# A GRU over 256 steps: the output product in one piece of 256 columns, ahead of the loop's jump

## The chip, the cores and the metric

The kernel runs on one core of a Trainium2 chip. The metric is the device time of one execution in microseconds. All data are fp32.

## What is computed

A recurrence over T = 256 steps for B = 32 sequences with C = 256 channels, and a residual:

```python
def step(H, xs):
    xz, xr, xh = xs
    Z = sigmoid(xz + H @ Whz.T + bhz)
    R = sigmoid(xr + H @ Whr.T + bhr)
    H_tilda = tanh(xh + R * H @ Whh.T + bhh)
    H_new = Z * H + (1.0 - Z) * H_tilda
    Y = H_new @ Whq.T + bhq
    return (H_new, Y)
# xz, xr, xh: x @ Wx.T + bx for the gates z, r and h, of every step
_, Ys = scan(step, h0, (Xz, Xr, Xh))
out = x + transpose(Ys, (1, 0, 2))
```

## The kernel before

States are held transposed, channels on the 128 partitions in K = 2 halves and 32 sequences along the free axis (h_sb, rh_sb, zh_sb, u_sb, z_sb). Steps are taken in chunks of CS = 2. The loop runs NIT = 64 times over SLOTS = 4 steps, u = 0 to 3, that is two chunks, p = 0 and 1; s is the step in the chunk (even steps s = 0, odd steps s = 1). PSUM banks hold the sums before the nonlinearity: r_ps and c_ps (two each), z_ps and y_ps (one for each p). ScalarE seeds each with its bias (seed, seed_y), TensorE adds products to it.

In a step (names as in the code): r is the sigmoid of r_ps (L182), rh = r * h on VectorE (L232), z the sigmoid of z_ps (L186), zh = z * h (L237), the tanh of c_ps (L193), u = (1 - z) * tanh (L240), the new h = zh + u (L245).

Every product is cut in four strips of 32 output rows (`columns`, L254, and `y_piece`): four matmuls with 128 x 32 weights at tile_position (0, 32 j) that lie side by side in the array. What TensorE gets is, in each step:

- r of this step. As h = zh + u, the parts (k, o) of `Whr h` are taken by distributivity: three parts from zh at the end of the step before (AHEAD), three from u as soon as it is there, and the last from h. A part is a half k of the input by a half o of the output. The first step of the loop, u = 0, is different: only one part comes from zh and one from u, three from h.
- z from h (16 matmuls), c from rh (16 matmuls, behind the waits s_rh).
- x pieces: the x products of the *next* chunk, moving 64 columns (two steps). 12 for a chunk, six in each step: one of the gate N ahead of z, one N and one Z ahead of c, one Z and two R behind c.
- the r parts from zh for the step to come (behind the wait s_zh).
- a y piece: one half k of the output product of the *last* chunk, both steps of it. Here h is the stationary operand and whq_sb moves with 128 columns. Its four strips are half and step: partitions are (half of C, step, sequence), columns 128 channels. Both pieces add up in PSUM.

The loop's jump stands behind the y piece of u = 3. VectorE adds y_ps and the rows of x (xres_sb) to o_sb in even steps, ahead of zh (`residual`, L219), and SP sends o_sb out and fetches new x and new rows. y_ps is seeded by ScalarE in odd steps between z and tanh (L190). Everything is ordered by hand; each engine runs its own copy of the loop, and semaphores link them.

## Time and profile before

| | us |
|---|---|
| median of 3 runs | 521.46 (520.5 to 522.43) |
| profiled execution | 522.41 |
| its span, first to last instruction | 520.6 |

| engine | busy us | share |
|---|---|---|
| TensorE matmuls | 508.4 | 98% |
| TensorE weight loads | 491.0 | 94% |
| ScalarE | 322.4 | 62% |
| VectorE | 306.6 | 59% |

DMA moves 53 GB/s in the mean. The chain of work that ended last is 96% TensorE. Matmuls are pipelined and their ends are modelled, so their starts are to be read rather than their durations: a matmul record is 0.19 to 0.29 us long, while the next four start a few hundredths of a microsecond later. A line of the timeline is a run of like instructions; its second number is the time from the first start to the last end.

### The profile page before, as it was taken

To read this page: it belongs to the slowest core of one execution; us is meant where nothing else is said; L and a number is where in the kernel's file an instruction comes from. 1 tells how busy PE (TensorE), PEld (TensorE's weight loads), DVE (VectorE), ACT (ScalarE), POOL (GpSimd) and SP (SyncE) were. 2 spreads that over 40 slices of the span, in tenths; PEclk is the share of its full clock that TensorE was granted. 3 is DMA by queue.
4 is the path that set the end of the run, shared out by engine and by line. 5 is a ranking of instruction groups with operands and counts; after the bars stand their busy time and mean duration, and the time that the engine had idled before them with its cause. 6 is when DMAs were issued, how large, how long until landed. Compare 5 with 4: busy or idle time off the path is not lost.

```text
span 520.6 us, 96194 instructions
## 1 busy us (share of the span) xinstructions
PE 508.4 (98%) x44184; PEld 491.0 (94%) x44184; DVE 306.6 (59%) x1929; ACT 322.4 (62%) x1800; POOL 0.2 (0%) x4
## 2 busy tenths in 40 slices
PE   8499999999999999999999999999999999999997
PEld 7499999999999999999999999999999999999997
DVE  1256666666666666666566666666666666665664
ACT  2256666666666666666666666666666666666664
POOL 0000000000000000000000000000000000000000
PEclk9989999999999999999999999999999999999999
DMA  5011111111111111111211111111111111111111
GB/s 182 25 45 49 52 51 50 51 50 50 50 50 50 52 49 50 55 46 50 55 46 50 55 47 50 54 50 50 51 50 50 50 50 50 50 50 52 49 50 52
DMA packets 57737, 27.64 MB, mean 53 GB/s; under 512 B 6785, under 2 KB 56833, under 8 KB 57729
## 3 DMA queue, kind: packets, MB, share of 16 engines
q1 hardware_dynamic: 56880, 26.70, 18.3%
q10 hardware_dynamic: 848, 0.83, 0.5%
q8 instruction: 6, 0.10, 0.1%
q14 instruction: 3, 0.02, 0.0%
HBM read 18.98 MB, written 8.52 MB: 53 GB/s over the span
## 4 chain that ended last, share of the span: by engine, by line
PE 96%; issue 2%; DMA 1%; SPq 0%; DVE 0%; ACT 0%; ACTq 0%; DVEq 0%
PE r_ps L252 34%; PE c_ps L252 27%; PE z_ps L252 24%; PE y_ps L252 11%; DMA whq_sb<-in_whq_dram 1%; SPq L117 0%; SPq L119 0%; SPq L118 0%; SPq L115 0%; DVE h_sb L245 0%; DVE o_sb L219 0%; DVE rh_sb L232 0%; DVE u_sb L240 0%; ACT c_ps L193 0%; ACT y_ps L182 0%
## 5 line engine op out<-in xcount | busy, mean ns | idle before, releaser
L252 PE MATMUL c_ps<-xt_sb,wx_sb 128*32 128x64 f32 (+1 forms) x4104 | 174.4, 225 | 1.3 <-issue 1.3
L252 PE MATMUL z_ps<-xt_sb,wx_sb 128*32 128x64 f32 (+1 forms) x4104 | 168.1, 221 | 0.5 <-issue 0.5
L232 DVE TENSOR_TENSOR rh_sb<-y_ps,h_sb 128x32 f32<-128x32 f32 x512 | 89.7, 192 | 130.0 <-ACT y_ps L182 130.0
L182 ACT ACTIVATE y_ps<-r_ps 128x32 f32<-128x32 f32 x512 | 87.3, 182 | 98.4 <-PE r_ps L252 92.2
L252 PE MATMUL z_ps<-h_sb,whz_sb 128*32 128x32 f32 x8192 | 124.2, 198 | 2.2 <-issue 2.2
L252 PE MATMUL c_ps<-rh_sb,whh_sb 128*32 128x32 f32 x8192 | 123.0, 198 | 2.0 <-issue 1.9
L252 PE MATMUL y_ps<-whq_sb,h_sb 128*32 128x128 f32 x2064 | 112.2, 278 | 0.2 <-DVE h_sb L245 0.2
L252 PE MATMUL r_ps<-xt_sb,wx_sb 128*32 128x64 f32 (+1 forms) x4104 | 112.3, 220 | 0.0
L252 PEld LDWEIGHTS z_ps<-h_sb,whz_sb 128*32 128x32 f32 x8192 | 109.0, 111 | 2.4 <-issue 2.4
L252 PEld LDWEIGHTS c_ps<-rh_sb,whh_sb 128*32 128x32 f32 x8192 | 103.5, 110 | 2.3 <-issue 2.0
L252 PEld LDWEIGHTS z_ps<-xt_sb,wx_sb 128*32 128x32 f32 (+1 forms) x4104 | 104.6, 110 | 0.7 <-issue 0.7
L252 PEld LDWEIGHTS r_ps<-u_sb,whr_sb 128*32 128x32 f32 x5120 | 86.1, 112 | 15.9 <-DVE u_sb L240 15.9
L252 PEld LDWEIGHTS c_ps<-xt_sb,wx_sb 128*32 128x32 f32 (+1 forms) x4104 | 98.1, 108 | 1.5 <-issue 1.5
L252 PE MATMUL r_ps<-zh_sb,whr_sb 128*32 128x32 f32 x5120 | 94.0, 197 | 1.9 <-issue 1.9
L252 PE MATMUL r_ps<-u_sb,whr_sb 128*32 128x32 f32 x5120 | 94.4, 197 | 0.3
L252 PEld LDWEIGHTS r_ps<-xt_sb,wx_sb 128*32 128x32 f32 (+1 forms) x4104 | 84.3, 110 | 0.2 <-issue 0.2
L252 PE MATMUL r_ps<-h_sb,whr_sb 128*32 128x32 f32 x3080 | 82.7, 199 | 0.0
L252 PEld LDWEIGHTS r_ps<-zh_sb,whr_sb 128*32 128x32 f32 x5120 | 75.1, 112 | 2.0 <-issue 2.0
L237 DVE TENSOR_TENSOR zh_sb<-z_sb,h_sb 128x64 f32<-128x64 f32 x256 | 57.0, 223 | 31.0 <-ACT z_sb L186 30.9
L245 DVE TENSOR_TENSOR h_sb<-zh_sb,u_sb 128x32 f32<-128x32 f32 x512 | 75.0, 187 | 0.0
L186 ACT ACTIVATE z_sb<-z_ps 128x64 f32<-128x64 f32 x256 | 57.2, 223 | 27.3 <-PE z_ps L252 27.0
L240 DVE SCALAR_TENSOR_TENSOR u_sb<-z_sb,c_ps 128x32 f32<-128x32 f32 x256 | 48.0, 188 | 39.2 <-ACT c_ps L193 32.9
(29 smaller groups left out, 438.1 us busy)
## 6 DMA issues: line engine op xcount, KB each, us to landing
xt_sb<-in_xt_dram SPq DMA_DIRECT2D x130, 64.0 KB, 1.7
xres_sb<-in_xr_dram SPq DMA_DIRECT2D x130, 64.0 KB, 1.8
out_dram<-o_sb SPq DMA_DIRECT2D x130, 64.0 KB, 1.6
wx_sb<-in_wx_dram SPq DMA_DIRECT2D x3, 256.0 KB, 3.2
whr_sb<-in_whr_dram ACTq DMA_DIRECT2D x1, 256.0 KB, 5.3
whz_sb<-in_whz_dram ACTq DMA_DIRECT2D x1, 256.0 KB, 5.5
...
```

Of the source, the lines that this page charges most:

```text
L182: nc.scalar.activation(r_out[p][o], r_ps[:, o, here], ACT.Sigmoid).then_inc(s_r[o], 1)
L186: nc.scalar.activation(z_sb[:], z_view(p)[:, :, B * s:B * s + B], ACT.Sigmoid).then_inc(s_z, 1)
L232: nc.vector.tensor_tensor(rh_sb[:, k], r_out[p][k], old[:, k], ALU.mult).then_inc(s_rh[k], 1)
L237: nc.vector.tensor_tensor(zh_sb[:], z_sb[:], old, ALU.mult).then_inc(s_zh, 1)
L240: nc.vector.scalar_tensor_tensor(u_sb[:, k], z_sb[:, k], 1.0, c_out[p][k], ALU.subtract, ALU.mult, reverse0=True).then_inc(s_u[k], 1)
L245: nc.vector.tensor_tensor(new[:, k], zh_sb[:, k], u_sb[:, k], ALU.add).then_inc(s_h[k], 1)
L252: return nc.tensor.matmul(ps, weights, moving, start=start, stop=False, skip_group_check=True, **kw)
```

## The change

y of a chunk is made once, in the odd step, by four matmuls with 256 moving columns (`y_rows`). The strips are now half k of h and step: the two halves' sums lie on the partitions 0 to 63 and 64 to 127 of y_ps, rows (step, sequence), columns all 256 channels. VectorE adds them in two operations of 64 x 256: the first half and the rows of x in the even step (behind rh, ahead of zh), the second half in the odd step. bq_sb, xres_sb, o_sb and the DRAM tensors change their shapes with it; bq is zero on the second half's partitions, and its transfer grows from 64 to 128 KB. ScalarE's seed of y moves behind the tanhs of even steps.

TensorE's order: y stands ahead of the r parts from zh in odd steps. At u = 3 it is the last thing before the jump, and the r parts from zh come behind the jump, at the head of the loop, behind a semaphore of their own (s_zh_pass). The step u = 0 splits r as the others do. x pieces are dealt out 8 to the even and 4 to the odd step.

```diff
+ROWS = CS * B
-AHEAD = [((1, 0),)] + [((0, 0), (1, 0), (1, 1))] * (SLOTS - 1)
+AHEAD = ((0, 0), (1, 0), (1, 1))
+AT_R = ((N, 0),), ((N, 2),)
+AT_Z = ((N, 1), (Z, 0)), ((N, 3), (Z, 3))
+AT_N = ((Z, 1), (Z, 2), (R, 0), (R, 1), (R, 2)), ((R, 3),)
...
 # ScalarE
-                return nc.scalar.copy(y_ps[p][:, 0, 0:P], bq_sb[:])
+                return nc.scalar.copy(y_ps[p][:, 0, 0:C], bq_sb[:])
...
-            seed_y(1).then_inc(s_seed_y, CS)
...
-                    if s == CS - 1:
-                        act.wait_ge(s_rh[1], t + 1)
-                        seed_y(p).then_inc(s_seed_y, CS)
                     for o in range(K):
                         act.wait_ge(s_c_ps[o], t + 1)
                         nc.scalar.activation(c_out[p][o], c_ps[:, o, here], ACT.Tanh).then_inc(s_c[o], 1)
-                    if s == CS - 1:
+                    if s == 0:
+                        act.wait_ge(s_res, t + CS)
+                        seed_y(1 - p).then_inc(s_seed_y, CS)
+                    else:
...
+            act.wait_ge(s_res, T + CS)
+            seed_y(1).then_inc(s_seed_y, CS)
...
 # VectorE
+            def residual_half0(p, row_dmas):
                 dve.wait_ge(s_rows[p], row_dmas)
-                dve.wait_ge(s_y_ps, chunk + PAD + 1)
-                nc.vector.tensor_tensor(o_sb[:, p], y_ps[p][:, 0, 0:P], xres_sb[:, p], ALU.add).then_inc(s_res, CS)
+                nc.vector.tensor_tensor(o_sb[:, p], y_ps[p][0:ROWS, 0, 0:C], xres_sb[:, p], ALU.add).then_inc(s_half, CS)
+
+            def residual_half1(p, count):
+                dve.wait_ge(s_half, count)
+                nc.vector.tensor_tensor(o_sb[:, p], y_ps[p][ROWS:P, 0, 0:C], o_sb[:, p], ALU.add).then_inc(s_res, CS)
...
 # TensorE
+            def y_rows(p):
                 for j in range(NQ):
-                    half, step = divmod(j, CS)
-                    last = mm(y_ps[p][B * j:B * j + B, 0, 0:P], h_sb[:, k, CS * p + step], whq_sb[:, k, P * half:P * half + P],
+                    k, step = divmod(j, CS)
+                    last = mm(y_ps[p][B * j:B * j + B, 0, 0:C], h_sb[:, k, CS * p + step], whq_sb[:, k],
                               tile_position=(0, B * j))
...
                     if u == 0:
-                        pe.wait_ge(s_u[1], done)
-                        r_part(u, 1, 0, u_sb[:, 1])
-                        pe.wait_ge(s_h[0], done)
-                        r_part(u, 0, 0, old[:, 0]).then_inc(s_r_ps[0], 1)
-                        r_part(u, 0, 1, old[:, 0])
-                        pe.wait_ge(s_h[1], done)
-                        r_part(u, 1, 1, old[:, 1]).then_inc(s_r_ps[1], 1)
-                    else:
...
+                        pe.wait_ge(s_zh_pass, done)
+                        for k, o in AHEAD:
+                            r_part(u, k, o, zh_sb[:, k])
...
                     if s == CS - 1:
                         x_mm.then_inc(s_xt_used, 1)
-                    pe.wait_ge(s_zh, done)
-                    for k, o in AHEAD[(u + 1) % SLOTS]:
-                        r_part((u + 1) % SLOTS, k, o, zh_sb[:, k])
-                    if s == 0:
                         pe.wait_ge(s_seed_y, done)
-                    y_mm = y_piece(q, s)
-                    if s == CS - 1:
-                        y_mm.then_inc(s_y_ps, 1)
+                        y_rows(q).then_inc(s_y_ps, 1)
+                    if u < SLOTS - 1:
+                        pe.wait_ge(s_zh, done)
+                        for k, o in AHEAD:
+                            r_part(u + 1, k, o, zh_sb[:, k])
```

What this does to TensorE's row round the jump: first the head of the loop (u = 0, up to the first x piece), then, behind the "...", its end (u = 3, from the c matmuls of rh's second half on). Before:

```order
L252 MATMUL r_ps<-u_sb,whr_sb 32x32 [waits s_u1]
L252 MATMUL r_ps<-u_sb,whr_sb 32x32 x3
L252 MATMUL r_ps<-h_sb,whr_sb 32x32 [waits s_h0]
...
L252 MATMUL c_ps<-rh_sb,whh_sb 32x32 x7
L252 MATMUL z_ps<-xt_sb,wx_sb 32x64 x4
L252 MATMUL r_ps<-xt_sb,wx_sb 32x64 x8
L252 MATMUL r_ps<-zh_sb,whr_sb 32x32 [waits s_zh]
L252 MATMUL r_ps<-zh_sb,whr_sb 32x32 x3
L252 MATMUL y_ps<-whq_sb,h_sb 32x128 x4
L314 REGISTER_ALU
L314 COMPARE_AND_BRANCH
```

The same places of TensorE after the change:

```order
L279 MATMUL r_ps<-zh_sb,whr_sb 32x32 [waits s_zh_pass]
L279 MATMUL r_ps<-zh_sb,whr_sb 32x32 x11
L279 MATMUL r_ps<-u_sb,whr_sb 32x32 [waits s_u0]
L279 MATMUL r_ps<-u_sb,whr_sb 32x32 x3
L279 MATMUL r_ps<-u_sb,whr_sb 32x32 [waits s_u1]
...
L279 MATMUL c_ps<-rh_sb,whh_sb 32x32 x7
L279 MATMUL r_ps<-xt_sb,wx_sb 32x64 x4
L279 MATMUL y_ps<-whq_sb,h_sb 32x256 [waits s_seed_y]
L279 MATMUL y_ps<-whq_sb,h_sb 32x256 x3
L341 REGISTER_ALU
L341 COMPARE_AND_BRANCH
```

The r parts of zh, 12 now, have moved from ahead of y over the jump, and two x pieces have left the end of u = 3.

VectorE in the steps u = 0 and u = 1, from rh to zh. Before:

```order
L232 TENSOR_TENSOR rh_sb<-y_ps,h_sb 128x32 [waits s_r1]
L217 ISA
L218 ISA [waits s_rows0]
L219 TENSOR_TENSOR o_sb<-y_ps,xres_sb 128x128 [waits s_y_ps]
L237 TENSOR_TENSOR zh_sb<-z_sb,h_sb 128x64 [waits s_z]
...
L232 TENSOR_TENSOR rh_sb<-y_ps,h_sb 128x32 [waits s_h1,s_r1]
L237 TENSOR_TENSOR zh_sb<-z_sb,h_sb 128x64 [waits s_z]
```

VectorE at the same places after the change:

```order
L246 TENSOR_TENSOR rh_sb<-y_ps,h_sb 128x32 [waits s_h1,s_r1]
L230 ISA
L231 TENSOR_TENSOR o_sb<-y_ps,xres_sb 64x256 [waits s_rows0]
L261 TENSOR_TENSOR zh_sb<-z_sb,h_sb 128x64 [waits s_z]
...
L246 TENSOR_TENSOR rh_sb<-y_ps,h_sb 128x32 [waits s_h1,s_r1]
L235 TENSOR_TENSOR o_sb<-y_ps,o_sb 64x256 [waits s_half]
L261 TENSOR_TENSOR zh_sb<-z_sb,h_sb 128x64 [waits s_z]
```

A residual operation stands ahead of zh in every step now, and the wait for y_ps is gone.

## Rows read from the trace of the kernel before

**Rows 1.** The page: busy time, GB/s by slice, the transfer out (KB, us to landing).

```profile
PE 508.4 (98%) x44184; PEld 491.0 (94%) x44184; DVE 306.6 (59%) x1929; ACT 322.4 (62%) x1800; POOL 0.2 (0%) x4
GB/s 182 25 45 49 52 51 50 51 50 50 50 50 50 52 49 50 55 46 50 55 46 50 55 47 50 54 50 50 51 50 50 50 50 50 50 50 52 49 50 52
out_dram<-o_sb SPq DMA_DIRECT2D x130, 64.0 KB, 1.6
```

**Rows 2.** Timeline, ScalarE: start us, us, operation, count [idle before].

```profile
284.48 0.34 ACT L182 ACTIVATE y_ps<-r_ps 128x32 f32<-128x32 f32 x2
...
285.52 0.18 ACT L193 ACTIVATE z_ps<-c_ps 128x32 f32<-128x32 f32 x1
...
290.26 0.34 ACT L182 ACTIVATE y_ps<-r_ps 128x32 f32<-128x32 f32 x2 [0.68 <-PE r_ps L252]
...
292.23 0.34 ACT L182 ACTIVATE y_ps<-r_ps 128x32 f32<-128x32 f32 x2
```

**Rows 3.** Timeline, TensorE's matmuls, end of the step u = 2.

```profile
289.23 0.43 PE L252 MATMUL r_ps<-xt_sb,wx_sb 128*32 128x64 f32 x16
289.45 0.38 PE L252 MATMUL r_ps<-zh_sb,whr_sb 128*32 128x32 f32 x23
289.64 0.31 PE L252 MATMUL y_ps<-whq_sb,h_sb 128*32 128x128 f32 x2
...
289.86 0.38 PE L252 MATMUL r_ps<-u_sb,whr_sb 128*32 128x32 f32 x21
```

**Rows 4.** Waits, TensorE's weight loads: us in total, times, longest us.

```profile
PEld r_ps L252 <- DVE u_sb L240: 15.9, 63, 0.3
```

**Rows 5.** Timeline, TensorE's matmuls round the jump from u = 3 to u = 0.

```profile
291.43 0.29 PE L252 MATMUL y_ps<-whq_sb,h_sb 128*32 128x128 f32 x2
...
291.83 0.27 PE L252 MATMUL r_ps<-u_sb,whr_sb 128*32 128x32 f32 x8
...
292.11 0.32 PE L252 MATMUL c_ps<-xt_sb,wx_sb 128*32 128x64 f32 x7
```

**Rows 6.** Timeline, TensorE's weight loads round the same jump.

```profile
291.43 0.16 PEld L252 LDWEIGHTS y_ps<-whq_sb,h_sb 128*32 128x32 f32 x6
291.83 0.16 PEld L252 LDWEIGHTS r_ps<-u_sb,whr_sb 128*32 128x32 f32 x8 [0.24 <-DVE u_sb L240]
```

**Rows 7.** Timeline, VectorE, steps u = 0 and u = 3.

```profile
285.12 0.29 DVE L219 TENSOR_TENSOR o_sb<-y_ps,xres_sb 128x128 f32<-128x128 f32 x1
285.33 0.21 DVE L237 TENSOR_TENSOR zh_sb<-z_sb,h_sb 128x64 f32<-128x64 f32 x1
...
290.48 0.35 DVE L232 TENSOR_TENSOR rh_sb<-y_ps,h_sb 128x32 f32<-128x32 f32 x2 [0.44 <-ACT y_ps L182]
...
291.43 0.19 DVE L240 SCALAR_TENSOR_TENSOR u_sb<-z_sb,c_ps 128x32 f32<-128x32 f32 x1 [0.17 <-ACT c_ps L193]
291.53 0.18 DVE L240 SCALAR_TENSOR_TENSOR u_sb<-z_sb,z_ps 128x32 f32<-128x32 f32 x1
```

**Rows 8.** The chain that ended last: start us, us, what.

```profile
3.56 6.72 DMA whq_sb<-in_whq_dram
...
35.40 0.44 PE r_ps L252 x32
...
493.93 0.46 PE r_ps L252 x32
```

**Rows 9.** Timeline, TensorE's matmuls at u = 0.

```profile
285.36 0.43 PE L252 MATMUL r_ps<-xt_sb,wx_sb 128*32 128x64 f32 x16
285.60 0.40 PE L252 MATMUL r_ps<-zh_sb,whr_sb 128*32 128x32 f32 x24
```

**Rows 10.** Timeline, the end of the kernel on ScalarE, TensorE and VectorE.

```profile
517.28 0.26 ACT L154 COPY z_ps<-b_sb 128x128 f32<-128x128 f32 x1
...
517.47 0.64 PE L252 MATMUL y_ps<-whq_sb,h_sb 128*32 128x128 f32 x16 [0.23 <-DVE h_sb L245]
...
518.27 0.29 DVE L219 TENSOR_TENSOR o_sb<-y_ps,xres_sb 128x128 f32<-128x128 f32 x1 [0.57 <-PE y_ps L252]
```

**Rows 11.** Timeline, ScalarE at the start.

```profile
10.38 0.27 ACT L160 COPY y_ps<-bq_sb 128x128 f32<-128x128 f32 x1 [4.47 <-DMA whq_sb<-in_whq_dram]
```

**Rows 12.** Busy time by stretch: stretch, us, PE, PEld, DVE, ACT, POOL, granted clock, DMA.

```profile
27.00:28.00 1.00, 1.00 (x77) 1.00 (x71) 0.78 (x4) 0.46 (x3) 0.00 (x0) 0.50 0.23 66
```

98 lines of the change are left out of this document (52 added, 46 removed).

## The prediction

> **What bounds the kernel now.** The page's busy shares come first: TensorE is busy 98% of the span [rows 1]. That is a hint only, so look next at who starts when. The r sigmoids open the steps for ScalarE and give the beat: from u = 0 at 284.48 to u = 3 at 290.26 it is 5.78 us, three steps of 1.93; from there over the loop's jump to u = 0 at 292.23 it is 1.97 [rows 2]. That step is the longest although it holds 20 r matmuls where the others hold 28. Inside a step TensorE's groups follow without a hole: the next starts when the one before has had its time. From such starts come the prices. Every fp32 matmul is two instructions in the trace, and four strips of 32 columns of the array run side by side, so four instructions make one pass:
> - 32 moving columns: 24 instructions in 0.19 us (289.45 to 289.64), 0.032 a pass;
> - 64 columns: 16 in 0.22 (289.23 to 289.45), 0.055 a pass;
> - 128 columns: the y piece, 8 in 0.22 (289.64 to 289.86), 0.11 a pass [rows 3].
>
> So the array's time is what counts, and a step is longer than it only where the array is left empty. The list of waits names one such place: weight loads of r_ps idle 15.9 us in 63 waits, 0.25 each, put down to VectorE's u_sb [rows 4]. Taken jumps are 63 too. The rows round one show that u_sb is not the cause: its second half is written by 291.71 (291.53 + 0.18), the first load comes at 291.83. The last load of y starts no later than 291.48 (its group ends at 291.59, each lasts 0.11) [rows 6, 7]. The 0.35 between is the jump. In the array y starts at 291.43 and r at 291.83: 0.40 where y alone needs 0.22, so 0.18 stays empty [rows 5]. The mean jump is a little worse: the chain has r groups at 35.40 and at 493.93, 59 iterations of 7.77 each [rows 8], and this iteration takes 7.75. I take 0.19.
>
> A small second hole lies at u = 0. Its 16 x matmuls of r take 0.24 (285.36 to 285.60), not 0.22, since the r parts of zh wait for zh, which ends at 285.54; zh is late there as the residual starts only at 285.12 [rows 7, 9].
>
> **The change, part by part.** An iteration is four steps, there are 64.
>
> *Jump.* y, now two passes of 256 columns, stands last before the jump, and the r parts of zh first behind it. From the first y matmul to the first load behind the jump it took 0.40 [rows 5, 6]. The new y keeps the array busy for 0.43 (below), and zh ends long before. So the hole closes, but for slow jumps. Gain 63 x 0.19 = **-12.0**; I leave 0.01 a jump, **+0.6**, and between 0 and 0.05 (3.2) for the range.
>
> The Trainium skill speaks against this: "TensorE: Matmul & The Clock Gate", Part 3, "The mechanism", says that weight loads overlap matmuls in flight only when they go to another row group. By it the second pass's loads of y, all on 128 rows, would wait for the first pass. The trace disagrees: six loads of y stand at 291.43 to 291.59, with the first y matmul, and the second pass is not due before 291.54 [rows 5, 6]. What would follow if it held for the long form is worked out as the second rival.
>
> *r parts.* Step 0 is made like the others: 12 matmuls of zh, 12 of u, 4 of h, where it was 4, 4 and 12. That is two parts of 8 instructions more. A part costs 0.063 (0.19 for three [rows 3]) to 0.07 (the four at 291.83 to 292.11 [rows 5]). 2 x 0.065 x 64 = **+8.3**.
>
> *y.* Four pieces of 0.22 an iteration become two of two passes of 256 columns. No row has 256 fp32 columns. Twice the 128-column pass is 0.22; from the step between 32 and 64 columns (0.023) one gets 0.11 + 4 x 0.023 = 0.20. I take 0.215, by the 128-column row, the nearest in size. So 0.43 for 0.44 a chunk: 128 x -0.01 = **-1.3** (0 to -5).
>
> *x pieces.* Two a chunk move from the odd step to the even one, behind the c matmuls, 4 x 0.055 = 0.22 there and back; none is added. Ahead of the c matmuls two pieces still stand in every step, the cover for rh. Nothing.
>
> *zh's wait at u = 0.* The moved pieces give zh 0.22 more; the hole of 0.02 goes: **-1.3**.
>
> *VectorE.* Every step now has a residual of 64 x 256 where every second had 128 x 128. By columns: 0.29 for 128; an operation of 32 takes 0.19 [rows 7]; so 0.10 for 96 columns, 0.13 for 128 more, 0.42. That fewer partitions make it cheaper no row shows; twice 0.29, 0.58, is the dear end. At u = 0 zh then ends at 285.67 instead of 285.54, and the r matmuls of zh come at 285.58 + 0.22 = 285.80. At u = 3 rh ends at 290.83, the residual runs to 291.25, zh (0.21, overlapped by 0.08 as at 285.33) to 291.38, while r's zh parts come behind y, which starts two x pieces (0.22) before 291.43 and takes 0.43: 291.64. So 0.13 and more cover at both, and u (291.43) starts when it did. Nothing; it decides from about 0.55 on. Added waits (s_h at u = 0, s_half) are for VectorE's own earlier results.
>
> *ScalarE.* y's seed is now a copy of 256 columns (0.27 for 128 [rows 11]; a tanh of 32 takes 0.18, so about 0.39) behind the tanhs of even steps, which end at 285.70; it ends near 286.09, 0.3 before the next step's sigmoid (284.48 + 1.93) [rows 2]. Nothing.
>
> *SP's queue* issues the same 64 KB transfers. The one of out follows a step later; the slot is written again a whole iteration after its first half, some 5.8 us after the issue, and the transfer lands in 1.6 [rows 1]. Nothing.
>
> *Start.* bq grows from 64 to 128 KB ahead of whq: up to 0.35 at the page's 182 GB/s [rows 1]. ScalarE waits for whq, which lands at 10.28, and then copied y's seed before the loop [rows 8, 11]: the copy (0.2 of it uncovered) leaves that place. **+0.15** (-0.2 to +0.35).
>
> *End.* y's last seed stands behind ScalarE's last copy, which ends at 517.54 [rows 10]: with 0.39 the last y starts at 517.95, not 517.47. Behind it two residuals of 0.42, overlapped by 0.08, for one of 0.29. 0.48 + 0.47 = **+1.0** (0.5 to 1.3).
>
> Sum: -12.0 + 0.6 + 8.3 - 1.3 - 1.3 + 0.15 + 1.0 = -4.5 us. The profiled execution took 522.41 (span 520.6 and 1.8 round it), 0.95 over the median of 521.46; it should go to 517.9, the median to **517.0**.
>
> **Rivals.** (1) The jump is covered in part. Behind it loads and matmuls start together (291.83 both), and the wait on s_zh_pass stands there. At 0.05 empty instead of 0.01: +2.5, 519.5; at 0.08, 521.4. For it, the longest of the 63 waits, 0.3, is 0.05 over the mean. Against: the eight passes behind the jump take 0.28, near 8 x 0.032. 19%.
>
> (2) Slower, by one mechanism: the second pass's loads of the long y go out only when its first pass ends. The last load would start 0.22 + 0.05 behind y's start and the first behind the jump 0.35 later, at 0.62, where 0.43 is due: 0.19 empty, as today, with the new work to pay. 517.0 + 63 x 0.18 = 528.3. It decides from 0.08 empty a jump on. Against it, the loads at 291.43. 7%.
>
> (3) The change doesn't do what it says: one piece of 256 columns costs more than two of 128. At 0.24 a pass, 128 x 0.05 = 6.4: 523.4. 5%.
>
> (4) VectorE's residual takes 0.60, zh comes 0.05 late in 256 steps, +12.8: 529.8. 3%.
>
> **How the numbers follow.** My own case has 66%. Its spread: y -3.7 or +1.3, r parts 0.3 to 0.6, start and end 0.5, and the clock: TensorE's granted clock was 0.50, the level of 1.2 GHz, at 27 to 28 us [rows 12], and such a stretch may be missing or longer in the new first iterations, one or two us. So 514.8 to 519.3. The range takes in rival 1 to its end, **514.8 to 521.6**, with (2) to (4) outside. A measurement here can tell 0.5%, 2.6 us, from no change: faster is under 518.9, slower over 524.1. Of my 66, 3 lie above 518.9: faster 0.63. Within: those 3, rival 1's 19 and 4 of rival 3, 0.26. Slower: (2), (4) and 1 of (3), 0.11.
>
> **What would show it.** The waits of r_ps loads at the jump gone or under 0.05 each; the first r matmul behind the jump 0.43 to 0.45 after y's start; iterations of 7.67 for 7.77; y passes of 0.21 to 0.22; residuals of 0.42, with zh done before it is needed. It is wrong if the gap of the loads at the jump starts later as y grows (rival 2), if iterations come out over 7.72 (rival 1), or if VectorE releases r's zh loads (rival 4).

## The result: 31 us slower

| | kernel before | changed kernel |
|---|---|---|
| median of 6 runs each, us | 521.55 | 552.69 |
| lowest to highest, us | 520.50 to 522.97 | 551.22 to 554.42 |
| span of the profiled execution, us | 520.6 | 551.0 |

The ratio is 1.0587, 95% interval 1.0567 to 1.0606. The forecast was 517.0 with a range up to 521.6; it missed by 35.7 us, and by the sign.

Start, as for the kernel before, with the beat: the starts of the r sigmoids on ScalarE in the changed kernel (timeline; start us, us, operation, count, in brackets the idle time before it), which answer to [rows 2].

```profile
284.60 0.34 ACT L190 ACTIVATE y_ps<-r_ps 128x32 f32<-128x32 f32 x2 [0.37 <-PE r_ps L279]
...
286.52 0.49 ACT L190 ACTIVATE y_ps<-r_ps 128x32 f32<-128x32 f32 x2
...
288.71 0.34 ACT L190 ACTIVATE y_ps<-r_ps 128x32 f32<-128x32 f32 x2 [0.37 <-PE r_ps L279]
...
290.63 0.48 ACT L190 ACTIVATE y_ps<-r_ps 128x32 f32<-128x32 f32 x2
...
292.81 0.34 ACT L190 ACTIVATE y_ps<-r_ps 128x32 f32<-128x32 f32 x2 [0.37 <-PE r_ps L279]
```

The odd steps, from 284.60 and from 288.71, take 1.92 us, as forecast. The even ones, from 286.52 and from 290.63, take 2.19 and 2.18. The pair of r sigmoids in them lasts 0.49 instead of 0.34, so already the second half of r_ps comes 0.15 late. An iteration takes 8.21 us where 7.67 was forecast: 64 x 0.54 = 35 us. That is nearly the whole miss, and it is in the even steps alone.

What the forecast looked at is in order. The jump lies ahead of 294.13 (matmuls of TensorE, then VectorE, timeline; answering to [rows 5] and [rows 7]).

```profile
293.69 0.64 PE L279 MATMUL y_ps<-whq_sb,h_sb 128*32 128x256 f32 x8
294.13 0.38 PE L279 MATMUL r_ps<-zh_sb,whr_sb 128*32 128x32 f32 x23
```

```profile
287.15 0.41 DVE L231 TENSOR_TENSOR o_sb<-y_ps,xres_sb 64x256 f32<-64x256 f32 x1
287.51 0.23 DVE L261 TENSOR_TENSOR zh_sb<-z_sb,h_sb 128x64 f32<-128x64 f32 x1
...
289.30 0.43 DVE L235 TENSOR_TENSOR o_sb<-y_ps,o_sb 64x256 f32<-64x256 f32 x1
```

From y to the first r matmul behind the jump it is 0.44, y's own time, and VectorE's adds take 0.41 to 0.43 where 0.42 was forecast. Neither is late.

The list of waits leads astray here: it shows weight loads idle behind y, put down to VectorE (us in all, times, longest), but there the array is still at work on the long y.

```profile
PEld r_ps L279 <- DVE zh_sb L258: 16.4, 63, 0.3
...
PEld r_ps L279 <- DVE zh_sb L261: 10.8, 64, 0.2
```

The loss stands in no wait. The busy time by stretch shows it, if one reads the count and not the share. A weight load lasts 0.11 us in the records and overlaps its neighbours, so the share stays at 0.10 of 0.10 us even where loads are missing. Weight loads of the changed kernel from the r sigmoid of u = 2 (286.52): stretch, its length, busy time (instructions running in it), granted clock, DMA share, GB/s.

```profile
286.42:286.52 0.10, 0.10 (x20) 1.00 0.00 0
286.52:286.62 0.10, 0.10 (x16) 1.00 0.00 0
286.62:286.72 0.10, 0.09 (x10) 1.00 0.00 0
286.72:286.82 0.10, 0.10 (x12) 1.00 0.00 0
286.82:286.92 0.10, 0.10 (x20) 1.00 0.00 0
...
287.22:287.32 0.10, 0.10 (x18) 1.00 0.67 164
287.32:287.42 0.10, 0.10 (x13) 1.00 0.21 52
287.42:287.52 0.10, 0.10 (x13) 1.00 0.01 0
287.52:287.62 0.10, 0.10 (x20) 1.00 0.00 0
```

A stretch of 32-column passes has 20 to 24 loads in it. Twice the number falls to 10 to 13: once among z's loads from h_sb, once among c's loads from rh_sb. In the trace of single loads each such place is a gap of about 0.11 us (0.09 for the second) and then passes slower than their 0.032 us: behind the first gap four of 0.036 to 0.051, behind the second one of 0.056 and then 0.035 (means over the loop). Together that is 0.15 us for the first place and 0.11 for the second, 0.26 a chunk. No instruction waits there, the clock is 1.00, and no data move at the first. I call these two places the stops.

Two more lists belong to the result, though I read them only in the third round of experiments: SyncE's issues (timeline) and the landings (issues of the page: count, KB, median us from issue to landing), the latter answering to [rows 1].

```profile
285.79 0.52 SPq L140 DMA_DIRECT2D out_dram<-o_sb  x1
286.51 0.50 SPq L141 DMA_DIRECT2D xres_sb<-in_xr_dram  x1
287.21 0.43 SPq L138 DMA_DIRECT2D xt_sb<-in_xt_dram  x1
```

```profile
xres_sb<-in_xr_dram SPq DMA_DIRECT2D x130, 64.0 KB, 2.1
out_dram<-o_sb SPq DMA_DIRECT2D x130, 64.0 KB, 2.0
```

The two row transfers, out and the residual input, are now 64 partitions of 1024 B instead of 128 of 512 B. out's issue takes 0.52 us (0.36 before), the input's 0.50 (0.33), the input's follows out's after 0.72 (0.55), and out lands in 2.0 us instead of 1.6. Even the x chunk, still over 128 partitions, takes 0.43 to issue (0.33 before) where it follows the input at once, as here. And 0.80 us behind 285.79 is 286.59, 0.80 us behind 286.51 is 287.31: the stops.

### The profile page after: what moved, and what is told of

Read it like the earlier page. It is cut to its first block, busy times and chain, and to the rows that moved or that the text cites. A ratio compares the mean times of both kernels' runs of the same rounds, so it can differ in the third digit from the quotient of the medians.

```text
span 551.0 us, 96615 instructions
## 1 busy us (share of the span) xinstructions
PE 536.1 (97%) x44168; PEld 505.7 (92%) x44168; DVE 374.6 (68%) x2060; ACT 344.0 (62%) x1800; POOL 0.2 (0%) x4
## 4 chain that ended last, share of the span: by engine, by line
PE 95%; DMA 2%; issue 2%; SPq 1%; DVE 0%; ACT 0%; ACTq 0%; DVEq 0%
PE r_ps L279 33%; PE c_ps L279 28%; PE z_ps L279 25%; PE y_ps L279 10%; DMA whq_sb<-in_whq_dram 1%; DMA xres_sb<-in_xr_dram 0%; SPq L126 0%; DVE o_sb L235 0%; SPq L140 0%; ACT y_ps L190 0%; SPq L128 0%; SPq L127 0%; DVE o_sb L231 0%; SPq L124 0%; DVE rh_sb L246 0%
## 5 line engine op out<-in xcount | busy, mean ns | idle before, releaser
L279 PE MATMUL z_ps<-h_sb,whz_sb 128*32 128x32 f32 x8192 | 142.8, 199 | 2.4 <-issue 2.3
L279 PE MATMUL z_ps<-xt_sb,wx_sb 128*32 128x64 f32 (+1 forms) x4104 | 141.9, 221 | 0.0
L279 PE MATMUL c_ps<-rh_sb,whh_sb 128*32 128x32 f32 x8192 | 137.6, 199 | 2.2 <-issue 2.1
L279 PEld LDWEIGHTS z_ps<-h_sb,whz_sb 128*32 128x32 f32 x8192 | 126.0, 110 | 3.3 <-issue 2.4
L279 PEld LDWEIGHTS c_ps<-rh_sb,whh_sb 128*32 128x32 f32 x8192 | 120.1, 110 | 2.5 <-issue 2.2
L279 PEld LDWEIGHTS r_ps<-zh_sb,whr_sb 128*32 128x32 f32 x6144 | 88.6, 112 | 29.8 <-DVE zh_sb L258 16.4
L279 PE MATMUL r_ps<-u_sb,whr_sb 128*32 128x32 f32 x6144 | 109.9, 200 | 1.4 <-issue 1.4
L197 ACT ACTIVATE c_ps<-c_ps 128x32 f32<-128x32 f32 x256 | 46.6, 182 | 71.7 <-PE c_ps L279 68.8
L279 PE MATMUL y_ps<-whq_sb,h_sb 128*32 128x256 f32 x1032 | 82.8, 380 | 0.8 <-ACT y_ps L169 0.8
L279 PE MATMUL r_ps<-h_sb,whr_sb 128*32 128x32 f32 x2048 | 70.7, 198 | 0.0
```

What stands on the lines that cost most here:

```text
L197: nc.scalar.activation(c_out[p][o], c_ps[:, o, here], ACT.Tanh).then_inc(s_c[o], 1)
L279: return nc.tensor.matmul(ps, weights, moving, start=start, stop=False, skip_group_check=True, **kw)
```

## The experiments

Times are medians, each with the ratio to runs of the kernel before on the same chip. The step lengths in the table at the end of this section are means over 60 iterations, from one r sigmoid's start to the next.

### First round: is it y's form, the deal of x, or the missing y pieces?

**y as two halves of 128 columns at the same place.**

```diff
-                for j in range(NQ):
-                    k, step = divmod(j, CS)
-                    last = mm(y_ps[p][B * j:B * j + B, 0, 0:C], h_sb[:, k, CS * p + step], whq_sb[:, k],
-                              tile_position=(0, B * j))
+                for half in range(2):
+                    cols = slice(P * half, P * half + P)
+                    for j in range(NQ):
+                        k, step = divmod(j, CS)
+                        last = mm(y_ps[p][B * j:B * j + B, 0, cols], h_sb[:, k, CS * p + step], whq_sb[:, k, cols],
+                                  tile_position=(0, B * j))
```

> The changed kernel with y written at the same place as two halves of 128 moving columns (16 instructions instead of 8, the same columns in all). Theory supply (the loads and matmuls of TensorE come late in the steps u=0 and u=2 because no y piece stands any more between their zh and u parts, so that long rows of 32-column passes run without relief): the two stops in each even step stay, 550 to 556 us. Rival wide piece (a 256-column matmul itself makes the later stops): they go, 515 to 520 us. VectorE's halves are the same in both.

Measured: 556.74 us, ratio 1.0657 (1.0628 to 1.0685), a little above the supply theory's range. The wide matmul is not the cause. One thing didn't fit the supply theory either: the stops moved by some loads against the program's text, and one now lay just ahead of the r sigmoid.

**x pieces six and six.**

```diff
-AT_Z = ((N, 1), (Z, 0)), ((N, 3), (Z, 3))
-AT_N = ((Z, 1), (Z, 2), (R, 0), (R, 1), (R, 2)), ((R, 3),)
+AT_Z = ((N, 1), (Z, 0)), ((N, 3), (Z, 2))
+AT_N = ((Z, 1), (R, 0), (R, 1)), ((Z, 3), (R, 2), (R, 3))
```

The wait for r's seed moves with its first piece.

> The changed kernel with the twelve x pieces dealt six and six to the two steps of a chunk, as the kernel before has them, instead of eight and four; y stays in one piece in the odd step. Rival deal (the uneven deal of x pieces makes the stops): even steps back at 1.90 us, 515 to 520 us. Theory supply: two x pieces more ahead of y give a little more relief in the odd step, none between zh and u; the stops stay, perhaps shorter, 535 to 555 us.

Measured: 567.04 us, ratio 1.0862 (1.0830 to 1.0893), slower than either theory said; why it is 14 us slower than the changed kernel was not traced. The deal is not the cause. The stops now lie at the end of the odd steps, 53 to 55 loads behind y, where it was 75 to 77 in the changed kernel. If the stream simply ran dry by count, this number should not change.

**y with 32 columns.**

```diff
-                    last = mm(y_ps[p][B * j:B * j + B, 0, 0:C], h_sb[:, k, CS * p + step], whq_sb[:, k],
+                    last = mm(y_ps[p][B * j:B * j + B, 0, 0:B], h_sb[:, k, CS * p + step], whq_sb[:, k, 0:B],
```

> The changed kernel with y moving only 32 of the 256 columns, at the same place and with the same 8 instructions; the other columns of y are not computed, so it is a time only. Each chunk has 2 x 0.19 us less of TensorE work. Theory supply: the short passes give less relief, the stops in the even steps stay or grow: 0.38 us x 128 = 48 us less work at most, of which the longer stops take back a part, 520 to 545 us. Rival wide piece: no stops left, and 48 us less work on the way: 470 us.

Measured: 545.73 us, ratio 1.0453 (1.0425 to 1.0482), just above the supply theory's range. The stops stayed. Of 48 us of work taken away only 7 show in the time, and one reason lies beside the stops: from y's start to the next r matmul it is 0.43 us in the changed kernel, and with the short y still 0.33 at u = 1, where r's zh parts then wait for zh (they start 0.05 behind its end), and 0.42 at u = 3, where they wait for the jump (medians of 60). So the long y stands mostly in time that would be empty without it.

**The jump's order alone, in the kernel before.** The y piece of u = 3 stands ahead of the jump, zh's r parts behind it, and the r parts of u = 0 have the uniform order; a y piece is still in every step.

```diff
                     if u == 0:
...
+                        pe.wait_ge(s_zh_pass, done)
+                        for k, o in AHEAD:
+                            r_part(u, k, o, zh_sb[:, k])
...
-                    pe.wait_ge(s_zh, done)
-                    for k, o in AHEAD[(u + 1) % SLOTS]:
-                        r_part((u + 1) % SLOTS, k, o, zh_sb[:, k])
+                    if u < SLOTS - 1:
+                        pe.wait_ge(s_zh, done)
+                        for k, o in AHEAD:
+                            r_part(u + 1, k, o, zh_sb[:, k])
```

> The kernel before with only the order at the loop's jump changed: at u=3 its y piece stands ahead of the jump and the zh parts of the first step behind it, with the uniform order of the r parts; a y piece of 128 columns is still in every step, VectorE's residual is whole. Theory supply: the steps u=1, 2, 3 keep their y piece between zh and u and keep their length; u=0 has none between and may stop (up to +0.28 us x 64 = +18 us), against 12 us less at the jump and the r parts' +8: 505 to 530 us. Rival wide piece, rival deal: no stops, 510 to 520 us. VectorE side theory: no stops, the same.

Measured: 531.54 us, ratio 1.0180 (1.0152 to 1.0207), above every range given. No stop in any step, also not in u = 0, which has no y piece between its zh and u parts. The 9 us are the two r parts more (8.3 in the forecast), with the jump as open as before: its 0.33 us in the loads outlast a y piece of 0.22. u = 3 takes 2.09 us for 1.98.

### Second round: the supply theory measured by itself

**A stretch of passes ahead of the loop.**

```diff
+            wide(12)
+            narrow(120)
+            wide(2)
+            narrow(60)
+            wide(4)
+            narrow(60)
+            wide(12)
+            narrow(60)
+            mid(24)
+            narrow(60)
+            mid(8)
+            narrow(60)
```

wide, mid and narrow are passes of 256, 64 and 32 columns, 4 loads and 4 matmuls each.

> The kernel before with a stretch of matmuls and weight loads put ahead of the loop (nothing waits inside it, results unused): 12 passes of 256 columns, then 120 passes of 32 columns (a pass is 4 loads and 4 matmuls), 2 wide, 60 narrow, 4 wide, 60 narrow, 12 wide, 60 narrow, 24 passes of 64 columns, 60 narrow, 8 of 64, 60 narrow. Theory supply: the narrow passes begin at 32 ns each and after some number of them stop for about 0.1 us and go on at 40 ns or more, since the instructions come slower than 4 ns each; a wide stretch ahead gives back a number of quick passes that grows with it up to a cap. Rival data (the stops come from waits of the recurrence, memory or transfers of the loop): all narrow passes take 32 ns to the end. The loop itself is as before, so the time is 521.5 us plus the stretch's own 20 to 25 us.

Measured: 576.69 us in one execution. The stretch took 55 us instead of 20 to 25, in part at the lower clock (0.50 at 19 to 23 us). Matmuls of the stretch (timeline):

```profile
19.07 1.93 PE L252 MATMUL y_ps<-wx_sb,whr_sb 128*32 128x32 f32 x128 [2.62 <-issue]
22.52 2.68 PE L252 MATMUL y_ps<-wx_sb,whr_sb 128*32 128x32 f32 x128 [1.52 <-issue]
26.25 1.93 PE L252 MATMUL y_ps<-wx_sb,whr_sb 128*32 128x32 f32 x128 [1.05 <-issue]
...
44.88 1.56 PE L252 MATMUL y_ps<-wx_sb,whr_sb 128*32 128x32 f32 x128 [2.04 <-issue]
```

and from its list of queues (packets, MB):

```profile
q8 instruction: 21, 0.34, 0.2%
```

where the kernel before and the changed one have

```profile
q8 instruction: 6, 0.10, 0.1%
```

Both theories missed something larger. Code that runs for the first time comes in blocks of 128 matmuls and 128 loads, 256 instructions, and 1 to 2.7 us pass between two blocks. The blocks start 3.4 to 4.0 us apart, whatever passes they hold and at either clock. The stretch has 482 passes of 8 instructions, 15 blocks, and the instruction queue has 15 packets more (0.34 MB for 21: 16 KB each). Inside a block at full clock the narrow passes behind a pause begin at 0.032 us; behind the eighth come one of 0.035 and one of 0.044, and then they go on at 0.033 to 0.034. So there is a small supply effect, 0.001 us a pass, and nothing like a stop of 0.11. In the loop no instruction packet arrives after the first pass through it (6 in all), so the stops there are not this either. The Trainium skill ("Runtime: NRT & Kernel Launch", Instruction fetch mechanics) names blocks of 16 KiB with 256 instructions, with which the trace agrees; it calls the cost of a block's border mostly hidden, and here it was not.

**The changed kernel with its jump order undone**, y in one piece between the zh and the u parts of the odd steps (DVE's and PE's handling of zh as in the kernel before):

```diff
-                    if s == CS - 1:
-                        pe.wait_ge(s_seed_y, done)
-                        y_rows(q).then_inc(s_y_ps, 1)
-                    if u < SLOTS - 1:
-                        pe.wait_ge(s_zh, done)
-                        for k, o in AHEAD:
-                            r_part(u + 1, k, o, zh_sb[:, k])
+                    pe.wait_ge(s_zh, done)
+                    for k, o in AHEAD[(u + 1) % SLOTS]:
+                        r_part((u + 1) % SLOTS, k, o, zh_sb[:, k])
+                    if s == CS - 1:
+                        pe.wait_ge(s_seed_y, done)
+                        y_rows(q).then_inc(s_y_ps, 1)
```

> The changed kernel with its order at the jump undone: y stays one 256-column piece in the odd steps only, but stands between the zh parts and the u parts, and the jump is crossed behind it, as in the kernel before (its order of the r parts in the first step as well). Theory supply: what matters is where the relief lies, not that the even steps have no y: in the even steps TensorE now waits for u behind the zh parts, and the load stream gains lead there, so no stop of 0.1 us in any step; 528 to 542 us (0.13 us more per odd step because 0.43 us of y stand ahead of the u parts where 0.22 and a wait of 0.085 us stood). Rival (a y piece is needed in every step): stops in the even steps as in the changed kernel, 550 to 560 us.

Measured: 564.05 us, ratio 1.0796 (1.0767 to 1.0825). Neither theory had it. No gap of 0.1 us stands 0.8 us behind an issue (at most 0.06, in the median), although the row transfers still go over 64 partitions; which parts of the lost time are waits and which are stops was not taken apart. The odd steps wait for zh, since only one x piece is left ahead of it, and carry all of y behind that wait. I had not priced this, and the run decides nothing on the stops.

### Third round: the row transfers

What was left as a common mark of the stops was time. I set the stops of all runs against every other event: their distance to SyncE's issues is the same in the changed kernel, with two halves and with six and six x pieces, 0.78 to 0.83 us behind the issue of out and behind that of the residual input, while the distance to y, to the r sigmoid and in loads varies. So the suspect became what the forecast had passed over.

**The kernel before with the changed kernel's row transfers**, from and to tiles of their own (so the sums of VectorE are not sent out; only the time counts):

```diff
-                    sp.dma_start(out[c], o_sb[:, p]).then_inc(s_rows[p], DMA)
-                    sp.dma_start(xres_sb[:, p], xr[c + PAD]).then_inc(s_rows[p], DMA)
+                    sp.dma_start(out[c].rearrange("(r a) c -> r (a c)", a=2), o_64[:, p]).then_inc(s_rows[p], DMA)
+                    sp.dma_start(xres_64[:, p], xr[c + PAD].rearrange("(r a) c -> r (a c)", a=2)).then_inc(s_rows[p], DMA)
```

> The kernel before with its row transfers (out and the residual input) given the changed kernel's shape, 64 partitions of 1024 B instead of 128 partitions of 512 B, from and to tiles of their own, so that the output holds zeros; all else as before. In the traces so far the stops of TensorE's load stream in the changed kernel lie 0.80 us behind the issue of a row transfer or 0.09 us behind it, and the issues are dearer (0.52 us instead of 0.36) and 0.72 us apart instead of 0.55. Theory shape: 64 x 1024 B issues do it wherever they lie: 540 to 555 us. Rival place (the issues now come later in the step and hit the 32-column passes of z and c, whatever their shape): the issues stay at 1.11 and 1.66 us of the even steps, 520 to 525 us. Theory supply (too few pauses for the instruction stream): nothing changed for it, 520 to 523 us.

**The changed kernel with the row transfers of before**, likewise from tiles of their own:

```diff
-                    sp.dma_start(out[c], o_sb[:, p]).then_inc(s_rows[p], DMA)
-                    sp.dma_start(xres_sb[:, p], xr[c + PAD]).then_inc(s_rows[p], DMA)
+                    sp.dma_start(out[c].rearrange("r (a c) -> (r a) c", a=2), o_128[:, p]).then_inc(s_rows[p], DMA)
+                    sp.dma_start(xres_128[:, p], xr[c + PAD].rearrange("r (a c) -> (r a) c", a=2)).then_inc(s_rows[p], DMA)
```

> The changed kernel with its row transfers given the shape of the kernel before, 128 partitions of 512 B, from and to tiles of their own (the output holds zeros; VectorE's two adds are as in the changed kernel). Theory shape: no stops, the even steps at 1.90 to 1.93 us, 515 to 520 us, the time predicted for the change. Rival place: the stops stay where the issues lie, 545 to 555 us. Theory supply: 550 to 553 us.

Measured: the changed kernel with 128-partition transfers 521.24 us, ratio 0.9966 (0.9949 to 0.9982), 1.2 us above the shape theory's range and far from the others. Its r sigmoids and SyncE's issues:

```profile
264.45 0.34 ACT L193 ACTIVATE y_ps<-r_ps 128x32 f32<-128x32 f32 x2 [0.36 <-PE r_ps L285]
...
266.38 0.34 ACT L193 ACTIVATE y_ps<-r_ps 128x32 f32<-128x32 f32 x2
...
268.31 0.34 ACT L193 ACTIVATE y_ps<-r_ps 128x32 f32<-128x32 f32 x2 [0.37 <-PE r_ps L285]
...
270.23 0.34 ACT L193 ACTIVATE y_ps<-r_ps 128x32 f32<-128x32 f32 x2
```

```profile
265.64 0.36 SPq L143 DMA_DIRECT2D out_dram<-o  x1
266.20 0.33 SPq L144 DMA_DIRECT2D xres<-in_xr_dram  x1
267.08 0.33 SPq L141 DMA_DIRECT2D xt_sb<-in_xt_dram  x1
```

All four steps take 1.92 to 1.93. The weight loads at the same place of the step as above, 0.84 to 1.14 us behind the issue of out:

```profile
266.48:266.58 0.10, 0.10 (x23) 1.00 0.40 128
266.58:266.68 0.10, 0.10 (x24) 1.00 0.98 302
266.68:266.78 0.10, 0.10 (x20) 1.00 0.68 200
```

No stop, although data now move at up to 302 GB/s at that very place, against 164 in the changed kernel's rows. So it is not the data rate.

The stop also holds matmuls that had started ahead of it. The last r matmul and the second r sigmoid of the step above, in the changed kernel and then with 128 partitions (timeline; for ScalarE from 286.71 and from 266.56, so that the pair is not one line):

```profile
286.42 0.20 PE L279 MATMUL r_ps<-h_sb,whr_sb 128*32 128x32 f32 x1
286.83 0.18 ACT L190 ACTIVATE y_ps<-r_ps 128x32 f32<-128x32 f32 x1
```

```profile
266.27 0.20 PE L285 MATMUL r_ps<-h_sb,whr_sb 128*32 128x32 f32 x1
266.54 0.18 ACT L193 ACTIVATE y_ps<-r_ps 128x32 f32<-128x32 f32 x1
```

From the matmul's start to the sigmoid that waits for it the even steps of the changed kernel take 0.41 and 0.40 us, with 128 or 32 partitions 0.26 (medians of 60). The matmul started in time and was done 0.14 late, so what stops is not only the supply of new instructions. The sigmoid itself takes 0.18 in both.

The kernel before with 64-partition transfers took 533.15 us, ratio 1.0198 (1.0168 to 1.0228): the shape alone harms it too, by 11 us, less than the 540 to 555 us expected of it. Its issues are at 1.1 and 1.8 us of the even steps. What lies 0.80 us behind out's is the end of the step, with an x piece, and no gap shows there; 0.80 behind the input's are c's loads from rh_sb in the odd step, which take 0.07 to 0.10 longer (2.03 and 2.05 us for 1.94 and 1.98). Its input issued at 284.48, then its weight loads:

```profile
284.48 0.50 SPq L136 DMA_DIRECT2D xres<-in_xr_dram  x1
```

```profile
285.20:285.30 0.10, 0.10 (x22) 1.00 0.67 144
285.30:285.40 0.10, 0.10 (x14) 1.00 0.12 31
285.40:285.50 0.10, 0.10 (x14) 1.00 0.00 0
```

Shape makes the stop, place makes its price.

**A whole version: 128 partitions, four small adds.** xres_sb, o_sb and the output are laid out as before, and each of VectorE's adds is split, as the halves of y lie on other partitions than their sum:

```diff
-                nc.vector.tensor_tensor(o_sb[:, p], y_ps[p][0:ROWS, 0, 0:C], xres_sb[:, p], ALU.add).then_inc(s_half, CS)
+                nc.vector.tensor_tensor(o_sb[0:ROWS, p], y_ps[p][0:ROWS, 0, 0:P], xres_sb[0:ROWS, p], ALU.add)
+                nc.vector.tensor_tensor(o_sb[ROWS:P, p], y_ps[p][ROWS:P, 0, P:C], xres_sb[ROWS:P, p], ALU.add).then_inc(s_half, CS)
```

> A whole version: the changed kernel with xres_sb, o_sb and the output again in 128 partitions of 512 B (the two column halves of a row in the two halves of the partitions), so that each of VectorE's two adds of 64 x 256 becomes two of 64 x 128; the output is complete. Theory shape: as f2, and VectorE's 4 x 0.25 us a chunk instead of 2 x 0.42 us stay hidden, 515 to 522 us. Rival place and theory supply: 545 to 555 us.

Measured: 556.84 us, ratio 1.0654 (1.0628 to 1.0680), outside both ranges. The stops are gone and a wait has come in their place. VectorE, and TensorE's loads:

```profile
284.42 0.29 DVE L236 TENSOR_TENSOR o_sb<-y_ps,o_sb 64x128 f32<-64x128 f32 x1
284.73 0.28 DVE L237 TENSOR_TENSOR o_sb<-y_ps,o_sb 64x128 f32<-64x128 f32 x1
285.05 0.23 DVE L260 TENSOR_TENSOR zh_sb<-z_sb,h_sb 128x64 f32<-128x64 f32 x1
...
285.32 0.28 PEld L281 LDWEIGHTS r_ps<-zh_sb,whr_sb 128*32 128x32 f32 x24 [0.46 <-DVE zh_sb L260]
```

Two adds on 64 partitions take 0.29 + 0.28 and do not overlap, 0.59 to the end instead of 0.42. I had priced them at 0.25 and called them hidden. It is the fourth rival of the forecast, a residual of 0.60, by another door: it put that at +12.8 us, and the loop alone lost 36 against 7.70.

**64 partitions, rows in two pieces of 512 B:** both tiles padded to 2 x 160 elements a row.

```diff
-        o_sb = sb("o_sb", [ROWS, 2, C])
+        o_sb = sb("o_sb", [ROWS, 2, K, P + B])
```

> A whole version: the changed kernel with both row tiles still on 64 partitions, but each row in two pieces of 512 B with a gap between them (o_sb and xres_sb padded to 2 x 160 elements), so that a row transfer consists of 128 pieces of 512 B as in the kernel before; VectorE's adds are 64 x 256 still. Theory piece size (the number of partitions doesn't matter, the pieces of 1024 B do): the stops go, the even steps take 1.92 to 1.93 us, 517 to 523 us. Theory partitions (a transfer over 64 partitions is what does it): stops as in the changed kernel, 548 to 556 us.

Measured: 550.08 us, ratio 1.0541 (1.0517 to 1.0566). The stops stay, 0.84 to 0.91 us behind each issue, and the issues are dearer still (0.61 and 0.56). The size of the pieces is not it.

**Only the residual input over 128 partitions.**

```diff
-                    sp.dma_start(xres_sb[:, p], xr[c + PAD]).then_inc(s_rows[p], DMA)
+                    sp.dma_start(xres_128[:, p], xr[c + PAD].rearrange("r (a c) -> (r a) c", a=2)).then_inc(s_rows[p], DMA)
```

> The changed kernel with the shape of 128 partitions of 512 B for the residual input alone (to a tile of its own, so the output lacks x); the output's transfer keeps 64 x 1024 B. Theory: every 64 x 1024 B transfer stops TensorE's loads once, 0.80 us behind its issue. Then the first stop of the even steps (0.80 us behind the output's issue) stays and the second (0.80 us behind the input's) goes: 0.13 to 0.15 us less in 128 steps, 530 to 538 us. Rival (the issues' spacing of 0.72 us, or one of the two transfers alone, makes both stops): 517 to 523 or 548 to 555 us.

Measured: 540.95 us, ratio 1.0365 (1.0337 to 1.0394), a little above the range. The stop among c's loads is gone in every step, that among z's (or just ahead of them) stays; where it falls ahead of the r sigmoid it lengthens the odd step instead of the even one (2.01 and 1.97 us). Each transfer has its own stop. The input's issue takes 0.44 us here although it goes over 128 partitions; it follows out's directly.

**32 partitions of 2048 B**, by the same edit with (r a) c -> r (a c).

> The changed kernel with its row transfers over 32 partitions of 2048 B, from and to tiles of their own (the output holds zeros; VectorE's adds as in the changed kernel). Theory partitions, graded (the fewer partitions one transfer has, the dearer its issue and the longer the stop behind it): both stops at least as long as with 64 partitions, issue of 0.52 us or more, 555 to 590 us. Rival (64 x 1024 B is a special case, or only a transfer's own length counts): 515 to 550 us.

Measured: 520.91 us, ratio 0.9963 (0.9948 to 0.9978). My graded theory fell: with 32 partitions there is no stop, and the issues take 0.34 to 0.35 and 0.32 us.

**The upper 64 partitions of tiles that nothing else uses.**

```diff
-                    sp.dma_start(out[c], o_sb[:, p]).then_inc(s_rows[p], DMA)
-                    sp.dma_start(xres_sb[:, p], xr[c + PAD]).then_inc(s_rows[p], DMA)
+                    sp.dma_start(out[c], o_up[ROWS:P, p]).then_inc(s_rows[p], DMA)
+                    sp.dma_start(xres_up[ROWS:P, p], xr[c + PAD]).then_inc(s_rows[p], DMA)
```

> The changed kernel with its row transfers over the partitions 64 to 127 of tiles of their own, 1024 B each (the output holds zeros; VectorE's adds as in the changed kernel). Theory (64 partitions in one transfer, wherever they lie): the stops of the changed kernel, issue at 0.52 us, 545 to 556 us. Rival (the lower half of the partitions, or the tiles that VectorE also writes and reads, matter): no stops, 517 to 523 us.

Measured: 553.82 us, ratio 1.0610 (1.0588 to 1.0632), the changed kernel over again. So it is neither the lower half of the partitions nor that VectorE works on the same tile.

### Versions that might beat both

**y in two 128-column pieces over all partitions, both ahead of the jump.** One add of 128 x 128, row transfers of before, the order of the changed kernel.

```diff
+                for k in range(K):
+                    for j in range(NQ):
+                        half, step = divmod(j, CS)
+                        last = mm(y_ps[p][B * j:B * j + B, 0, 0:P], h_sb[:, k, CS * p + step], whq_sb[:, k, P * half:P * half + P],
+                                  tile_position=(0, B * j))
```

> A whole version: the changed kernel's order (y of a chunk ahead of the jump, z h parts behind it, x pieces eight and four), but y as in the kernel before, two pieces of 128 columns over all 128 partitions, one behind the other in the odd step, with one residual add of 128 x 128 and row transfers of 128 partitions x 512 B. Theory partitions: no stops, all steps at 1.92 to 1.93 us as in the run with the changed kernel's y and 128-partition transfers, 517 to 523 us. Theory supply: as with two halves of y at the same place, 550 to 558 us.

Measured: 522.20 us, ratio 0.9993 (0.9978 to 1.0007), no difference from the kernel before. The steps are 1.93, 1.93, 1.92 and 1.97: only the last 128-column pass is still to run when the jump begins, and 0.04 of the jump stays open. Put beside the two halves of the first round, which have the same y time at the same place and 556.74 us, it shows once more that the order was never the trouble.

**Each row transfer as two over 32 partitions.**

```diff
+            def rows_out(p, rows):
+                for g in range(0, ROWS, B):
+                    sp.dma_start(rows[g:g + B], o_sb[g:g + B, p]).then_inc(s_rows[p], DMA)
```

> A whole version: the changed kernel with every row transfer over 64 partitions issued as two over 32 partitions each (1024 B a partition as before, 32 KB each), so SyncE issues five transfers a chunk instead of three. Theory (a single transfer over 64 partitions is what stops TensorE's loads; over 32 or 128 it doesn't): no stops, all steps at 1.92 to 1.93 us, 518 to 523 us. Rival (it is the amount of row bytes that goes to the partitions 0 to 63 in pieces of 1024 B or less): stops in the even steps, 545 to 560 us.

Measured: 539.02 us, ratio 1.0338 (1.0315 to 1.0362), outside both ranges. No stops, but a new wait (list of waits):

```profile
ACT c_ps L171 <- DMA xt_sb<-in_xt_dram: 31.1, 62, 0.7
```

Four row issues stand ahead of the next x chunk in SyncE's queue; it comes late, ScalarE's bias copy waits for it, and TensorE for that.

**SyncE asks for x first.** The order in the loop is turned so that x goes out as soon as its slot is free:

```diff
-                    sp.wait_ge(s_xt_used, c + 1)
-                    sp.dma_start(xt_sb[:, p], xt[c + 2 + PAD]).then_inc(s_xt[p], DMA)
+                    sp.wait_ge(s_xt_used, c + 2)
+                    sp.dma_start(xt_sb[:, 1 - p], xt[c + 3 + PAD]).then_inc(s_xt[1 - p], DMA)
```

> A whole version: two transfers over 32 partitions for every row transfer, as before, and SyncE's order turned, so that the x chunk is asked for as soon as TensorE has read the last one, ahead of the row transfers instead of behind them (there PE waited 0.25 us in every second step for the bias copy that waits for x). Theory: no stops and no late x, all steps at 1.92 to 1.93 us, 517 to 522 us. Rival (five issues a chunk are too many for SyncE in this place too): 525 to 540 us.

Measured: 523.65 us, ratio 1.0035 (1.0020 to 1.0049), a little above the range. The wait is gone and an iteration takes 7.73 us, worth 3 us against the kernel before; the end ate the gain. From the last r sigmoid to the end it is 8.8 us (5.0 before), as VectorE waits 2.58 us there for the last rows of the input.

> A whole version: the changed kernel with only SyncE's order turned as in the other run; its row transfers still go over 64 partitions in one. They are then issued about 0.4 us later, out at some 1.55 us of the odd step and the input 0.72 us behind it. Theory (a stop 0.80 us behind each 64-partition issue, which costs only where 32-column passes follow): the first stop moves to 0.4 us of the even step, by the x pieces between the parts of z and c, the second to 1.1 us, among the x pieces: even steps 1.93 to 2.00 us, 519 to 528 us. Rival (the stops cost the same wherever they lie): 545 to 555 us.

Measured: 536.84 us, ratio 1.0275 (1.0249 to 1.0301): half of the loss, between the two ranges. The issues lie some 0.35 us later than I had reckoned, so the stops land elsewhere than I wrote. out's falls among the x pieces of the even step and costs next to nothing. The input's, issued at 286.59, falls among the 32-column passes of r's zh parts (weight loads):

```profile
287.40:287.50 0.10, 0.10 (x14) 1.00 0.20 52
287.50:287.60 0.10, 0.10 (x8) 1.00 0.01 0
287.60:287.70 0.10, 0.10 (x19) 1.00 0.00 0
```

The rival, equal cost wherever the stops lie, is out.

| kernel | row transfer | u=0 | u=1 | u=2 | u=3 | iteration, us |
|---|---|---|---|---|---|---|
| before | 128 x 512 B | 1.94 | 1.94 | 1.91 | 1.98 | 7.77 |
| changed | 64 x 1024 B | 2.20 | 1.92 | 2.17 | 1.93 | 8.21 |
| y in two halves | 64 | 2.05 | 1.93 | 2.16 | 2.14 | 8.27 |
| x six and six | 64 | 1.95 | 2.26 | 1.94 | 2.27 | 8.41 |
| y of 32 columns | 64 | 2.21 | 1.86 | 2.14 | 1.90 | 8.10 |
| before, jump order only | 128 | 1.94 | 1.94 | 1.94 | 2.09 | 7.91 |
| y behind zh | 64 | 2.01 | 2.26 | 1.99 | 2.14 | 8.39 |
| before, 64 partitions | 64 | 1.94 | 2.03 | 1.91 | 2.05 | 7.94 |
| changed, 128 partitions | 128 | 1.93 | 1.92 | 1.92 | 1.92 | 7.70 |
| 128 and four small adds | 128 | 2.03 | 2.10 | 2.02 | 2.10 | 8.26 |
| 64 x 2 x 512 B | 64 | 2.19 | 1.92 | 2.12 | 1.93 | 8.15 |
| out 64, input 128 | both | 2.04 | 2.01 | 1.99 | 1.97 | 8.01 |
| changed, 32 partitions | 32 x 2048 B | 1.93 | 1.92 | 1.92 | 1.92 | 7.70 |
| changed, upper 64 | 64 | 2.20 | 1.92 | 2.16 | 1.93 | 8.21 |
| y 2 x 128 ahead of jump | 128 | 1.93 | 1.93 | 1.92 | 1.97 | 7.75 |
| two transfers of 32 | 2 x 32 | 1.95 | 2.13 | 1.97 | 1.93 | 7.99 |
| the same, x first | 2 x 32 | 1.96 | 1.92 | 1.93 | 1.92 | 7.73 |
| changed, x first | 64 | 2.04 | 1.92 | 2.05 | 1.92 | 7.93 |

## Why the prediction was wrong

The step that failed is the paragraph on SP's queue: "issues the same 64 KB transfers ... Nothing." They have the same size, and not the same shape. The diff changed xres_sb, o_sb and out from 128 partitions to 64, and I priced only when the transfers are issued, not what a transfer over 64 partitions is. With the changed kernel's own code and 128- or 32-partition transfers (from and to tiles of their own, so that the output is not complete) the ratio is 0.9966 or 0.9963; with 64 partitions it is 1.0587, and from tiles of their own 1.0610. That is shown from both sides, as the kernel before loses 11 us by the same shape. No rival had it. A residual of 64 x 256 got a term, a range and a rival; its transfers, changed by the same lines, got a sentence. By the forecast's own sign, iterations over 7.72, the jump would have been blamed; the starts round it clear it.

The other steps, held against the run with 128 partitions where the changed kernel hides them:

- **Jump:** right. 0.44 from y to the first r matmul behind it, forecast 0.43 to 0.45. No step at the jump is long. The first two rivals are out. So the row [rows 6] on loads beside the running y was read rightly.
- **y's price:** right, 0.216 us a pass of 256 columns, as taken. The run with 32 columns shows that it matters little: behind a y without length the r parts come only 0.10 and 0.02 us earlier.
- **r parts, zh, x pieces:** an iteration of 7.70 where 7.67 was forecast. The forecast's own terms give 7.68 (5.7 us less in 64 iterations); measured are 4.7 us less, from 7.77 to 7.70. All four steps take 1.92 to 1.93.
- **VectorE and ScalarE:** right in the loop. 0.42 us for the add, 0.38 for the copy of 256 columns (0.39), neither on the path. But the cover is thinner than the forecast's times say: in the odd steps zh ends 0.16 us ahead of the first r matmul that needs it, where 0.26 followed at u = 3.
- **End:** too small. From the last r sigmoid to the end it is 6.9 us with 128 or 32 partitions and 7.6 in the changed kernel, where the kernel before has 5.0; forecast +1.0. The last input transfer comes later than the last y, since out now goes out a step later and the input stands behind it in SyncE's queue: the sentence on SP's queue failed here too. The version with one add in the even step, whose out goes out there, has 5.3. (VectorE of the changed kernel; the second add follows 0.52 us behind this one, not overlapped as forecast.)

```profile
547.53 0.42 DVE L231 TENSOR_TENSOR o_sb<-y_ps,xres_sb 64x256 f32<-64x256 f32 x1 [1.27 <-DMA xres_sb<-in_xr_dram]
```

- **Start:** not settled. The second iteration ends 35.4 us behind the first instruction with 128 partitions, 37.4 with 32, 36.0 in the changed kernel and 35.8 in the kernel before. The first two have the same code but for the transfers, so one profile of each can't tell the 0.15 us of the forecast.

In all, the run with 128 partitions is 0.34% faster than the kernel before, 1.8 us (0.9 to 2.7), where the sum said 4.5. The iterations of its profile give 4.7 and the end takes back 1.9; the rest lies within what single executions differ by. Had the transfers kept their shape, the mechanism would have held with about two fifths of its gain, under the 2.6 us that the forecast had set for a change. No complete version shows this gain: the best one took 522.20 us.

What stays open is why 64 partitions in one transfer do this and 32 or 128 don't. Shown is that the issue itself takes longer (0.50 to 0.52 us against 0.32 to 0.36), that the landing is later, that the stop comes at a fixed distance behind the issue and ahead of the transfer's own data (out's first packet moves 1.18 us behind its issue; over 128 partitions 0.86, over 32 partitions 0.85), that it holds matmuls already started, and that neither the size of the pieces, nor the half of the partitions, nor the direction, nor sharing a tile with VectorE matters. The distance is closer still if it is counted from the end of the issue: 0.27 to 0.32 us in the median, in the changed kernel (issues of 0.52 and 0.50), with two pieces a row (0.61 and 0.56) and with out alone over 64 partitions (0.49). So a longer issue brings a later stop. Other numbers than 32, 64 and 128 were not tried, nor other queues than SyncE's.
